# Cross-attention on one Trainium2 core: in 22 of the 40 steps the output projection's first two chunks go in front of the values product, and its other three chunks move forward

## The reference

```python
q = _split_heads(hidden_states @ Wq.T, H)
k = _split_heads(text @ Wk.T, H)
v = _split_heads(text @ Wv.T, H)
out_text = _merge_heads(_attend(q, k, v, sm_scale))   # softmax(q k^T / sqrt(32)) v
...
out = out @ Wo.T + bo
return out + residual
```

## Time and profile before

| what | value |
| --- | --- |
| median of 3 runs | 427.18 us (426.95 to 427.48) |
| profiled execution, its own time | 427.04 us |
| span from its first to its last instruction | 425.2 us |
| TensorE matmul busy | 416.9 us, 98% |
| POOL, ACT, DVE busy | 306.2 us (72%), 301.0 us (71%), 263.1 us (62%) |
| mean granted TensorE clock | 0.999 |

### The profile page before, as it was taken

How to read it: one execution, slowest core, us unless ns; L and a number is a source line. 1 busy time by engine, 2 the same in 40 slices (tenths; PEclk the granted TensorE clock), 3 DMA queues, 4 the chain that set the end, 5 groups by cost and what they waited for, 6 DMA issues and landing times.

```text
span 425.2 us, 8268 instructions
## 1 busy us (share of the span) xinstructions
PE 416.9 (98%) x2550; PEld 238.9 (56%) x2550; DVE 263.1 (62%) x544; ACT 301.0 (71%) x584; POOL 306.2 (72%) x267
## 2 busy tenths in 40 slices
PE   8999999999999999999999999999999999999996
PEld 6877775677777755544444444444444444444442
DVE  0354676755676687776677656765677655556723
ACT  1638888857477788998767975888667966966720
POOL 8327799999659698798959594769649594764560
PEclk9999999999999999999999999999999999999999
DMA  8997636444844576454753347334743446345203
GB/s 270 371 345 244 229 114 217 158 155 145 280 156 156 186 259 207 158 169 143 257 184 125 134 149 243 126 135 174 248 166 127 148 150 222 132 167 192 84 25 125
DMA packets 41781, 77.33 MB, mean 182 GB/s; under 512 B 5264, under 2 KB 6416, under 8 KB 41744
## 3 DMA queue, kind: packets, MB, share of 16 engines
q1 hardware_dynamic: 30944, 57.21, 38.7%
q10 hardware_dynamic: 10800, 19.67, 14.3%
HBM read 33.40 MB, written 10.49 MB: 103 GB/s over the span
## 4 chain that ended last, share of the span: by engine, by line
PE 86%; ACT 3%; DMA 2%; issue 2%; DVE 2%; SPq 2%; POOL 1%; ACTq 0%; DVEq 0%; POOLq 0%
PE ps_q L928 28%; PE ps_o L928 27%; PE ps_s L993 9%; PE ps_pv L1000 7%; PE ps_m L979 5%; PE ps_den L1005 4%; PE ps_o L900 2%; DMA x_f<-in_x 2%; PE ps_m L1050 1%; PE ps_m L984 1%; SPq L367 1%; PE ps_q L1050 1%; PE ps_s L1050 1%; PE ps_o L1050 1%; ACT p_hi L584 1%
## 5 line engine op out<-in xcount | busy, mean ns | idle before, releaser
L449 POOL TENSOR_TENSOR p_lo<-p_f,p_hi 77x512 f16<-77x512 f32 x160 | 183.2, 1165 | 85.9 <-ACT p_hi L584 84.7
L580 ACT ACTIVATE p_f<-ps_s 77x512 f32<-77x512 f32 x160 | 94.3, 589 | 21.8 <-PE ps_s L993 20.7
L716 DVE TENSOR_REDUCE mx<-ps_m 128x4 f32<-128x308 f32 x160 | 69.2, 475 | 44.5 <-PE ps_m L979 43.6
L584 ACT ACTIVATE p_hi<-ps_s 77x512 f16<-77x512 f32 x160 | 93.5, 584 | 2.5 <-PE ps_den L1005 2.4
L928 PE MATMUL ps_o<-attn,wo 128*128 128x512 f16 x360 | 90.0, 381 | 0.4 <-DVE sums L791 0.2
L928 PE MATMUL ps_q<-x,wq 128*128 128x512 f16 x375 | 85.1, 379 | 0.0
L993 PE MATMUL ps_s<-q_packed,k_packed 128*77 128x512 f32 x160 | 63.4, 439 | 0.3
L928 PEld LDWEIGHTS ps_q<-x,wq 128*128 128x128 f16 x375 | 36.3, 98 | 44.5 <-issue 0.8
L928 PEld LDWEIGHTS ps_o<-attn,wo 128*128 128x128 f16 x360 | 31.2, 98 | 38.1 <-issue 6.6
L705 DVE SCALAR_TENSOR_TENSOR q_lo<-ps_q,q_scale,q_hi 128x512 fp32r<-128x512 f32 x25 | 18.8, 751 | 49.6 <-ACT q_hi L563 49.6
L979 PE MATMUL ps_m<-k_diag,q_hi 128*128 128x308 f32 x160 | 42.3, 344 | 0.6 <-ACT q_hi L563 0.6
(11 more groups left out here) (126 smaller groups left out, 661.9 us busy)
## 6 DMA issues: line engine op xcount, KB each, us to landing
q_packed<-q_hi SPq DMA_DIRECT2D x80, 256.0 KB, 2.5
x_f<-in_x SPq DMA_DIRECT2D x45, 256.0 KB, 4.3
q_packed<-q_lo SPq DMA_DIRECT2D x40, 256.0 KB, 3.3
x_res<-in_x ACTq DMA_DIRECT2D x35, 256.0 KB, 2.7
out<-x_res ACTq DMA_DIRECT2D x35, 256.0 KB, 2.7
wq_sb<-in_wq SPq DMA_DIRECT2D x10, 320.0 KB, 4.2
wo_sb<-in_wo SPq DMA_DIRECT2D x10, 320.0 KB, 4.0
wk_sb<-in_wk SPq DMA_DIRECT2D x8, 320.0 KB, 5.5
```

The source lines that it names most:

```text
L449: nc.gpsimd.tensor_tensor(p_lo[:, i, :], p_f[:, i, :], p_hi[:, i, :], ALU.subtract).then_inc(plo_done, 1)
L580: nc.scalar.activation(p_f[:, i, :], ps_s[i % 2][0:L, :], ACT.Exp, scale=SCALE).then_inc(pf_done, 1)
L584: nc.scalar.activation(p_hi[:, i, :], ps_s[i % 2][0:L, :], ACT.Exp, scale=SCALE).then_inc(phi_done, 1)
L716: nc.vector.tensor_reduce(mx[:, g % RS, :, tt], ps_m[tt % 2][:, 0:HG * L].rearrange("p (h k) -> p h k", k=L), AX_X, ALU.max).then_inc(max_ ...
```

## The change

In steps that have an output tile and no `sum_tops`, a new flag `early` puts chunks 0 and 1 of `project_out` in front of `values`. Chunk 2 stands where chunks 0 and 1 stood (between the maxima), chunks 3 and 4 where chunks 2 and 3 stood (between scores 2 and 3), and nothing stands where chunk 4 stood. These are steps 6 to 9, 19, 20, 22 to 25, 27 to 30 and 32 to 39: 22 steps, of which 21 have maxima. No instruction is added or removed, and the waits go with the pieces that they belong to.

```diff
                 if isinstance(t, int) and (t, g) == (1, 1):
                     pe.wait_ge(diag_done, HG * B)
+                early = bool(tiles) and not has_sums(t, g)
+                if early:
+                    project_out(*tiles[0], (0, 1))
                 values(last_t, last_g, batch(last_t))
                 if exists(t):
                     scores(t, g, 0, batch(t))
...
                 if tiles:
-                    project_out(*tiles[0], (0, 1))
+                    project_out(*tiles[0], (2,) if early else (0, 1))
                 if exists(max_t):
                     max_scores(max_t, max_g, 2, batch(max_t))
                     max_scores(max_t, max_g, 3, batch(max_t))
                 if exists(t):
                     scores(t, g, 2, batch(t))
                 if tiles:
-                    project_out(*tiles[0], (2, 3))
+                    project_out(*tiles[0], (3, 4) if early else (2, 3))
                 if exists(t):
                     scores(t, g, 3, batch(t))
                 if exists(max_t):
                     transpose_max(max_t, max_g)
-                if tiles:
+                if tiles and not early:
                     project_out(*tiles[0], (4,))
```

## The result

| kernel | median | range | ratio to before, 95% interval |
| --- | --- | --- | --- |
| before | 427.33 us, 4 runs | 426.95 to 427.53 | 1 |
| changed | 439.68 us, 4 runs | 439.39 to 440.21 | 1.0292 (1.0279 to 1.0304) |

The profiled execution of the changed kernel took 439.85 us, its span is 438.1 us, and its clock is at full level. On its page matmuls are as many as before, and TensorE is busy for 7 us more; the row of granted clock is the same as before.

What follows compares the result with a forecast made beforehand. The prediction took TensorE to be full. Its terms, 5.8 + 1.3 + 1.25 + 1.4 + 2.4 - 0.1 = 12.05 us, added to the profiled 427.04 us gave 439.1 us, range 435 to 443 us.

Steps and rivals of the forecast that it cites:

- the term of 0: Whole kernel: the same matmuls run, so their own time is worth 0.
- Item 1: Maxima 0 and 1 to maxima 2 and 3, 21 steps: TensorE waits for VectorE's second reduce, 5.8 us together.
- the sum of 436.8 us: Total if weight loads could also pass the wait on the reduce, the 21 stalls costing 3.5 us, not 5.8.
- Item 2: Step 6, attention operands: chunk 1 of the output projection waits for GpSimd's `attn_low`, 1.3 us.
- the clock falls: Rival: short TensorE gaps in early steps lower the clock; one step at 1.2 GHz gives 448.6 us; chance 0.02.
- Item 3: Step 19, weights: output projection waits for GpSimd's low half of its float16 weights, 1.25 us.
- Item 4: Step 36, attention operands: chunk 1 waits for GpSimd's operand, which moves about 1.07 us later; loss 1.4 us.
- Item 5: Step 39, output bank: output projection waits for VectorE's read of tile (6, 3)'s bank, delaying the values; 2.4 us.
- The signs: Next profile: TensorE waits over 1 us each in steps 6, 19, 36, 39; `mx` weight-load waits of 0.2 to 0.3.
- The spill-over: Shifted GpSimd or ScalarE stalls steps after 20, 25, 30: taken as 0; as rival up to 444.6 us, chance 0.05.

Runs made afterwards that it cites:

- the sums ahead of the scores: Kernel before, with sum_tops of the 12 steps with sums moved ahead of scores 0 and 1: 425.84 us, ratio 0.9969.
- both edits: Changed kernel with two chunks between the maxima again and steps 6, 19, 36 and 39 in the old order: 427.48 us, ratio 1.0010.

## Why the prediction was right

- *TensorE is full, so reordering gains next to nothing and waits are paid in full.* Right, for an order that only moves filler about. An order that takes away waits can gain: the sums ahead of the scores give 1.24 us, 0.3%, by waits that lie in steps that this change does not touch. With both edits 18 steps still have the new lead and the time is 427.48 us. So the lead by itself is worth nothing, as the term of 0 said.
- *Item 1, the maxima.* Right in place and size: 6.0 us against 5.8. With three matmuls taken away between them the waits come; with two chunks back in place they are gone. Steps 20 and 25 cost some 0.1 more than the rule, since the first reduce started later there (below). The weight of maximum 3 waits for the reduce, as in step 4. The Trainium skill says that weight loads are pulled ahead of matmuls in flight (TensorE: Matmul & The Clock Gate, Step-by-step: what each phase is for); a load that waits for a semaphore was not pulled ahead of that wait in any of the steps seen, and with that the sum of 436.8 us that I gave beside it falls.
- *Item 2, step 6.* 1.24 against 1.3. But the item lacked what the variants then showed: behind the waits of this step the clock falls in some executions. The rival "the clock falls" had 0.02 and a cause in the short gaps of each step, and its price was wrong too: it took a whole step at the lower level, 9.5 us, where a fall costs 2.0 to 4.0. The length of the eight first matmuls stood for the lower level there; the view of the clock shows full clock for them, so no row of the old kernel had the price of a fall. The changed kernel's four executions show no fall. The 18 executions of all kernels with this step's long wait have 6 with a clock of 0.991 or 0.992, and the 34 of the other variants and all runs of the kernel before have 0.998 or more. So the order of step 6 that the changed kernel has carries the hazard in three other kernels. Of their 14 executions with it 6 fell; at that share four executions in a row are spared about one time in nine. Whether the changed kernel was spared by luck or is less exposed is not shown. With a fall its time would have been near 443 us, at the edge of the range.
- *Item 3, step 19.* 1.25 as forecast. GpSimd's instruction didn't move, but for what the steps before it had grown by.
- *Item 4, step 36.* 1.46 against 1.4. That the operand moves with the scores of the step before, less ScalarE's old lateness, was right: chunk 1's ends 1.07 us later in the step, as worked out, and ScalarE's first exponential starts 1.06 later; with one chunk in front it grew by 0.67 where the same sum gave 0.6.
- *Item 5, step 39.* 2.3 against 2.4, and alone 2.4.
- *The signs.* The four places show the waits that were named, but not each over 1 us: step 36 has two of 0.83 and 0.31, and step 39 has 0.85 for `x_res`. The prediction speaks of three distances that shrink and lists five places.
- *The rest.* The spill-over taken as 0 in the steps behind 20, 25 and 30 is 0.00, 0.09 and 0.00 us. The reason given for 0 was not right, as the variant with both edits shows: there step 36 has the old order and its chunk 4 waits 0.19 us, and VectorE's `q_low`, which the prediction did not look at, is late in steps 21 and 26. No wait of the output projection for `finish_out` shows but that of step 39.

The sum was 12.05 us and the difference of the medians 12.35, 439.1 against 439.68 us. The other 0.3 us is the start of the sum: the profiled execution took 427.04 us, the median of the kernel before is 427.33. So the number is right because its terms are, each to 0.2 us, and the errors did not have to cancel.

## What to carry to other kernels

When one engine is full, an order of its work is a set of distances: for each buffer that is written again, and each operand made elsewhere, how much work lies between the result and its next use. Moving a filler block to the front leaves its old place thinner, and each distance across that place has to be read again from the trace; here three matmuls were too little between the uses of either pair of banks, unless the other pair's matmuls stood there too. Then look at the steps in which the moved block has inputs of its own, at the first tile, at a switch of weights and at the end: four such steps of 22 cost half of the loss.

## What the runs showed of the hardware

- A wait can cost more than its length by the clock. In step 6 TensorE ran matmuls for 1.46 of 3.2 us; then, in the one such execution that was traced, the granted clock was at 1.2 GHz for 6.6 us, and the step took 3.1 us more. Six executions of three kernels with that order have a lower mean clock, and they took 2.0 to 4.0 us more than the others of the same kernel. The program didn't decide which, since some executions of it fell and some didn't.
- At the head of steps 20 and 25 the first reduce of VectorE started some 0.12 us later behind the maxima than in other steps: in step 20 at 225.53, 0.47 after the first of them starts, in step 23 at 254.63, 0.34 after it starts. Step 20 is the first of VectorE's loop and step 25 opens its second turn, step 30 is outside the loop and has no delay. That the loop's own instructions cost this is my reading; no run here tells it apart. The old order has the same 0.47, 0.46 and 0.34 in steps 20, 25 and 23, and there it was hidden.
- A matmul that waits with its weights shows as busy. The gaps over 0.1 us in TensorE's row grew only by the one-off waits of steps 6, 19, 36 and 39 (and 0.2 in step 26). The maxima's 6.0 us are no idle time in the page: they are most of the rise in TensorE's busy time, 416.9 to 424.3 us, and appear as waits only in the view of weight loads.
